# Loading bias, gate and expert weights at other places of a graph and expert network on one core

## What is computed

```python
# layer 3: graph attention, 4 heads of 64 channels
out = agg.reshape(n, H * C) + bias          # agg: weighted sum over each node's edges
x = x + elu(out)
# layer 4: 8 experts, the 2 with the best gate scores of each node
xn = layernorm(x)
gate_scores = xn @ Wg + bg
_, idx = top_k(gate_scores, 2)
h = gelu(xn @ W1[e] + b1[e]); y = h @ W2[e] + b2[e]     # for both experts, summed
x = x + y
```

## Time and profile before

| | |
|---|---|
| time, median of 3 runs | 6628.99 us (6628.88 to 6632.55) |
| span of the profiled execution, first to last instruction | 6628.2 us |
| busy: TensorE, VectorE, ScalarE, GpSimd | 71%, 60%, 30%, 64% |
| attention pass, its bulk | 3300 to 5400 us |
| routing pass | 5426.6 to 5756 us |
| expert pass | from 5784 us |

### The profile page before, as it was taken

The page is one execution under the profiler, slowest core; times in us unless marked ns, Lnnn a source line. Parts: engine busy times, 40 slices in busy tenths (PEclk is TensorE's granted clock), DMA queues, the critical chain, the costliest instruction groups (busy, mean ns, idle before and its releaser), DMA issues. The chain is left out here.

```text
span 6628.2 us, 114498 instructions
## 1 busy us (share of the span) xinstructions
PE 4704.7 (71%) x25073; PEld 4033.2 (61%) x25073; DVE 3983.4 (60%) x11854; ACT 1982.2 (30%) x4950; POOL 4262.0 (64%) x4656
## 2 busy tenths in 40 slices
PE   9965555555555558599276777776766767599997
PEld 4445555555555556599265656565655557599996
DVE  5565555555555559522577777777777768644442
ACT  3310000000000006133144444444444434366664
POOL 1257777777777767255677777777777738544443
PEclk9987777777777779699677777767777775599998
DMA  8843333333333339111444444444444435444445
GB/s 313 319 168 105 104 104 104 104 105 105 104 104 104 105 102 306 44 63 63 146 114 113 113 114 113 113 113 113 114 113 113 113 117 181 143 71 72 72 71 129
DMA packets 376353, 810.49 MB, mean 122 GB/s; under 512 B 88803, under 2 KB 234803, under 8 KB 362453
## 3 DMA queue, kind: packets, MB, share of 16 engines
q0 software_dynamic: 209712, 525.20, 30.1%
q1 hardware_dynamic: 138836, 160.68, 7.7%
q10 hardware_dynamic: 27568, 122.44, 5.0%
HBM read 578.58 MB, written 242.27 MB: 124 GB/s over the span
## 5 line engine op out<-in xcount | busy, mean ns | idle before, releaser
L1259 POOL DMA_INDIRECT s_rows<-xp_table,s_index x1664 | 1654.5, 994 | 507.1 <-issue 449.8
L347 POOL DMA_INDIRECT s_rows<-rel_table,s_staged x1664 | 1580.1, 950 | 520.0 <-issue 496.5
L373 PE MATMUL s_part<-s_pick,s_rows 128*128 128x128 f32 x6656 | 1198.0, 354 | 903.5 <-DMA s_rows<-rel_table,s_staged 704.3
L373 PEld LDWEIGHTS s_part<-s_pick,s_rows 128*128 128x128 f32 x6656 | 1109.8, 260 | 992.3 <-DVE s_pick L381 919.0
L1383 PE MATMUL s_part<-s_pick,s_scaled 128*128 128x128 f32 x6656 | 1422.3, 371 | 378.4 <-DVE s_scaled L1548 351.1
L1383 PEld LDWEIGHTS s_part<-s_pick,s_scaled 128*128 128x128 f32 x6656 | 1192.6, 263 | 575.0 <-issue 277.8
L394 DVE TENSOR_TENSOR sums<-sums,s_part 128x256 f32 x1666 | 702.0, 421 | 933.9 <-PE s_part L373 754.8
L1563 DVE SCALAR_TENSOR_TENSOR sums<-sums,s_old_share,s_part 128x256 f32 x1666 | 793.6, 476 | 418.7 <-PE s_part L1383 281.2
L1295 ACT ACTIVATE s_apart<-window,s_local 128x128 f32<-128x128 f32 x1664 | 531.6, 390 | 1148.9 <-PE s_part L1383 1087.9
L1548 DVE TENSOR_TENSOR s_scaled<-s_rows,s_share 128x256 f32<-128x256 f32 x1664 | 687.5, 413 | 74.6 <-issue 73.5
L2291 POOL DMA_INDIRECT sums_out<-s_y,s_ids x212 | 334.0, 1575 | 485.7 <-DVE s_ids L2400 470.7
(11 more groups left out here) (357 smaller groups left out, 5486.8 us busy)
## 6 DMA issues: line engine op xcount, KB each, us to landing
rel_table<-s_rows ACTq DMA_DIRECT2D x98, 1024.0 KB
s_rows<-exp_rows SPq DMA_DIRECT2D x212, 132.0 KB, 2.1
s_rows<-rel_table,s_staged POOLq DMA_INDIRECT x1664, 2.7
s_rows<-xp_table,s_index POOLq DMA_INDIRECT x1664
s_edges<-edge_rows SPq DMA_DIRECT2D x208, 80.0 KB
xp_table<-s_xp ACTq DMA_DIRECT2D x49, 264.0 KB, 3.9
s_x<-in_x SPq DMA_DIRECT2D x98, 128.0 KB, 4.2
s_x<-in_x SPq DMA_DIRECT2D x49, 256.0 KB
```

The lines of the kernel that those rows point to most:

```text
L347: pool.indirect_dma_start(out=rows[:, s, :], out_offset=None, in_=rel_table[:, :], in_offset=bass.IndirectOffsetOnAxis(ap=staged[:, 2 * s ...
L373: mm = pe.matmul(part[s % PARTS][:, k, :], rows[:, s, k * P:(k + 1) * P], pick[:, s % PICKS, :], start=True, stop=True)
L1259: pool.indirect_dma_start(out=rows[:, b * BATCH + s, :], out_offset=None, in_=xp_table[0:NP, :], in_offset=bass.IndirectOffsetOnAxis(ap=in ...
```

## The change

Three small tiles (gate weights, gate bias, attention bias: 26 floats in each partition) are allocated before the attention pass and kept, in place of tiles of the routing pass. SP loads them in the attention pass's block, after its last `follow`, with ten DMAs, and waits there for them; the waits of ScalarE, TensorE and VectorE in the routing pass are gone. The expert weights are no longer issued ahead of the pairs: in pairs 2, 6, ..., 30 SP issues the two loads of one expert, behind the load of x2 and ahead of the store of x3, and in pair 34 the load of `b2`. The expert pass waits for 17 loads instead of 3.

```diff
         sums = at(ctx, "sums8", [P, HALVES, NP + P])
+        wg = at(ctx, "gate_w", [P, HALVES, X])
+        bg = at(ctx, "gate_b", [P, X])
+        bias = at(ctx, "att_bias", [P, HALVES])
...
+                    def load_front():
+
+                        run = CH // HALVES
+                        for h in range(HEADS):
+                            for k in range(HALVES):
+                                sp.dma_start(bias[h * run:(h + 1) * run, k:k + 1],
+                                             a["att_bias"][0:1, h * CH + k * run:h * CH + (k + 1) * run].rearrange("o c -> c o")).then_inc(front_in, 16)
+                        sp.dma_start(wg[:, :, :], a["gate_w"]).then_inc(front_in, 16)
+                        sp.dma_start(bg[:, :], a["gate_b"].broadcast_to([P, X])).then_inc(front_in, 16)
...
                     with sp.Fori(0, BATCHES // 2 - 1) as i:
                         follow(i, 0)
                         follow(i, 1)
+                    load_front()
+                    sp.wait_ge(front_in, 16 * (HEADS * HALVES + 2))
...
-                    part = CH // HALVES
-                    for h in range(HEADS):
-                        for k in range(HALVES):
-                            sp.dma_start(bias[h * part:(h + 1) * part, k:k + 1],
-                                         a["att_bias"][0:1, h * CH + k * part:h * CH + (k + 1) * part].rearrange("o c -> c o")).then_inc(bias_in, 16)
+                    def load_expert(e):
+                        sp.dma_start(w1_b1[:, e, :], a["exp_w1_b1"][:, e, :]).then_inc(exp_in, 16)
+                        sp.dma_start(w2[:, e, :], a["exp_w2"][:, e, :]).then_inc(exp_in, 16)
+
                     load(0)
                     load(1)
-                    sp.dma_start(wg[:, :, :], a["gate_w"]).then_inc(w_in, 16)
-                    sp.dma_start(bg[:, :], a["gate_b"].broadcast_to([P, X])).then_inc(w_in, 16)
-
-                    sp.dma_start(w1_b1[:, :, :], a["exp_w1_b1"]).then_inc(exp_in, 16)
-                    sp.dma_start(w2[:, :, :], a["exp_w2"]).then_inc(exp_in, 16)
-                    sp.dma_start(b2[:, :, :].rearrange("p x d -> p (x d)"), a["exp_b2"].broadcast_to([P, X * D])).then_inc(exp_in, 16)
                     for q in range(PAIRS):
                         if q + 2 < PAIRS:
                             sp.wait_ge(part_done, q + 1)
                             load(q + 2)
+                        if q % 4 == 2 and q // 4 < X:
+                            load_expert(q // 4)
+                        if q == 4 * X + 2:
+                            sp.dma_start(b2[:, :, :].rearrange("p x d -> p (x d)"), a["exp_b2"].broadcast_to([P, X * D])).then_inc(exp_in, 16)
                         sp.wait_ge(x3_done, q + 1)
...
-                    act.wait_ge(bias_in, 16 * HEADS * HALVES)
...
-                    pe.wait_ge(w_in, 32)
...
-                    v.wait_ge(w_in, 32)
...
-                    act.wait_ge(exp_in, 48)
+                    act.wait_ge(exp_in, 16 * (2 * X + 1))
...
-                    v.wait_ge(exp_in, 48)
+                    v.wait_ge(exp_in, 16 * (2 * X + 1))
```

More of the change, by code:

```diff
@@ L1168, in gnn_kernel @@
             gathered = [sem(f"s8_gathered{b}") for b in range(2)]
-            cleared = sem("s8_cleared")
+            cleared, front_in = sem("s8_cleared"), sem("s8_front_in")
             rows_scaled, apart_done, picked, product, added = (sem(f"s8_{n}") for n in ("rows_scaled", "apart_done", "picked", "product", "added"))
@@ L1761, in gnn_kernel @@
         with ExitStack() as st:
-            wg = at(st, "s9_wg", [P, HALVES, X])
-            bg = at(st, "s9_bg", [P, X])
-            bias = at(st, "s9_bias", [P, HALVES])
             x2 = at(st, "s9_x2", [P, 2, 2, D])
@@ L1794, in gnn_kernel @@
             psR = [bank(st, f"s9_psR{b}", 2, X) for b in range(2)]
-            w_in, bias_in = sem("s9_w_in"), sem("s9_bias_in")
             x_in, x3_out = [sem(f"s9_x_in{b}") for b in range(2)], [sem(f"s9_x3_out{b}") for b in range(3)]
```

## The result

The changed kernel takes 6606.82 us (median of six runs, 6603.35 to 6608.56); the kernel before takes 6629.86 us in the same measurement (six runs, 6624.70 to 6633.03). The ratio is 0.9965, 95% interval 0.9954 to 0.9977: faster by 0.35%, 23.0 us. Forecast were 22.3 us, and 6606.7 us as the time.

What follows compares the result with a forecast made beforehand. GpSimd was taken to bound the routing pass from its first scatter, so only that scatter's start counts: 5.1 (opening) + 17.2 (stall) + 0 (weights) = 22.3 us, 6629.0 - 22.3 = 6606.7 us; range 6602 to 6613.

Steps and rivals of the forecast that it cites:

- GpSimd as the bound, 5.8 us a pair: Routing pass from its first scatter on: GpSimd has no holes and sets the pace, 5.8 us a pair.
- Opening, 5.1 us: Start of the routing pass: no wait for bias and gate loads, VectorE's first add 5.1 us earlier (4.2 to 5.4).
- The second condition: VectorE's first add also needs x2 of pair 0, issued 4.24 us earlier and landing at 5428.7 to 5430.3.
- Stall, 17.2 us: Add of pair 2: the 18.13 us wait for x2 behind the expert weights goes, ScalarE is late next, gain 17.2 us.
- Weights beside the pairs, 0: Routing pass: expert loads among the pairs cost 0; one expert takes 5.9 us beside the steady traffic.
- lead: Loads of x2 in the routing pass: an expert can take about 13.3 us before VectorE waits.
- The other bound, 26 us of stretched issues: GpSimd's scatters: one issue in each of nine loads stretched by 2.9 us, 26 us in all; held unlikely.
- Small loads in the attention pass, 0: End of the attention pass: ten more issues, 5.3 us of an SP that then idles over 100 us, cost 0.
- Cut up: Rival, routing pass: each ninth of the weights delays its pair, only the opening's gain remains, 6623.9 us; chance 0.07.
- the opening gains nothing: Rival, start of the routing pass: ScalarE or x2 is late for another reason, 6611.8 us; chance 0.05.
- exposed in full: Rival, routing pass: pairs stand still for the small expert loads, 52 us, time 6659 us; chance 0.02.
- gathers by their address: Rival, attention pass: tile addresses move by about 100 bytes and stretch gathers, up to 78 us; chance 0.03 for well slower.

Runs made afterwards that it cites:

- kernel 8: Changed kernel with each inverse root computed a second time on GpSimd into an unread tile; 7924.1 us, ratio to the kernel before 0.9998.
- kernel 4: Changed kernel with all expert weights issued in pair 2 as seventeen loads; 8085.6 us, ratio to the kernel before 0.9983.
- kernel 10: Changed kernel with expert weights put back as three whole loads ahead of the pairs, run again on chip C; 8095.2 us, one run.
- kernel 12: The kernel before the change, unaltered, run again on chip C for a trace; 8095.8 us, one run.
- kernel 2: Kernel before with only the expert weights moved beside the pairs, bias and gate loads as before; 8081.8 us, ratio to the kernel before 0.9980.
- kernel 1: Changed kernel with expert weights put back as three whole loads ahead of the pairs, on chip A; 8088.5 us, ratio to the kernel before 0.9989.
- kernel 3: Changed kernel with all expert weights issued in pair 2 as three whole loads; 8082.6 us, ratio to the kernel before 0.9980.
- kernel 6: The changed kernel, unaltered, run again on chip B; 7898.6 us, ratio to the kernel before 0.9962.
- kernel 11: Changed kernel with the inverse root moved from GpSimd to ScalarE as exp of a logarithm; 8103.7 us, ratio to the kernel before 1.0014.

## Why the prediction was right, point by point

- **GpSimd as the bound, 5.8 us a pair: right.** Stretch 281.8 us after; kernel 8 lengthens it by 0.7 of the added work, with hardly any idle time filled.
- **Opening, 5.1 us: right in size, and the reason for the choice too.** The first add moved from 8.24 to 2.97 us after the first issue, 5.3 us. The second condition that the prediction named, x2 of pair 0, is now what it waits for (1.67 us), landing inside the forecast window of 5428.7 to 5430.3 counted from the old start. The page after now has a landing for these loads, 2.8 us at the median, between the two rows of 2.1 and 3.7 us that the forecast went by.
- **Stall, 17.2 us: right.** F - S fell by 22.5 us; less the opening's 5.3 this leaves 17.2. The add of pair 2 waits 0.88 us for ScalarE, 18.13 - 0.88 = 17.25. It is the stall minus what was late next that counts.
- **Weights beside the pairs, 0: right, though the lead was put too long.** 286.7 against 287.2 us on one chip, and 283.4 against 281.8 on the first. The DMA share is 0.70 in a window with weights, as forecast. There is a lead, and it has the order forecast: with 1.05 MB a burst no pair waits, with 4.2 MB one waits 3.6 us, with 9.45 MB 16.4. At pair 2 it is 10.0 us by the forecast's own reckoning and not 13.3, and a burst drains more slowly than at 424 GB/s. A burst of one expert is too short for either to matter. The other bound, 26 us of stretched issues, did not occur: the 196 scatters take 195.2 us in all, and took 196.8.
- **Small loads in the attention pass, 0: right.** SP issues them in 4.6 us, 109 us before the pass ends.
- **Rivals.** "Cut up" falls with the stretch; "the opening gains nothing" with the first add; "exposed in full" with the missing waits and with kernel 4, where seventeen loads cost 0.6 us of wait; "gathers by their address" with 993 for 994 ns. The block does start 0.5 us earlier than at 5426.6, which the prediction called a sign of the gathers; it is too little to bear on the verdict.
- **How near the number came is in part luck.** The 22.5 us of the first scatter fit the 22.3 of the sum. The 0.5, 1.6 and -1.1 us beside them were not forecast and mostly cancel, and the interval of the ratio allows 15 to 30 us.
- **What the prediction did not say:** that the two parts aren't independent. It adds 5.1 and 17.2 as though each stood alone. The sum is right for both together. For one alone the split is about 3 and 19: 3.0 us for the front (kernels 10 and 12, one run of a trace each) and 43.8 - 24.8 = 19.0 for the weights, of which the second number crosses chips.

Open: kernel 2's stretch is 298.2 us where kernel 1 on the same chip has 293.6. Its scatters aren't slower (199.9 us in all for 200.6); GpSimd is idle ahead of scatters and powers for 66.7 us instead of 61.6, 4.5 of these 5.1 us in waits for VectorE, and VectorE itself sits longer ahead of `s_counts` (32.9 us for 21.2). Chip C has such waits in the kernel before too (24.7 us), with no weights beside the pairs, and chip B shows no cost of the weights (286.7 to 287.2). One trace of each doesn't tell chance from a few us of contention on the slower chips. Also open is why the DMA engines ran at 369 GB/s in kernel 10 and at 384 in kernel 12.

## What to carry to other kernels

A small load that stands in a queue behind megabytes waits for all of them, whoever needs them. Compare a burst with the lead of the loads behind it (here 10 to 13 us, two pairs), count the traffic that goes beside it, and cut until it fits. Cutting finer cost little here: seventeen loads for three, 0.6 us of wait. When a stall goes, subtract what is late next. And when two edits sit on one chain, ask what each is worth alone: ahead of a wait for a transfer, work that is done earlier gains only what the end of the transfer gains.

## What the runs showed of the hardware

- **SP can be held in issuing.** Behind the expert weights one store took 7.8 us to issue (kernel 12), 9.8 (kernel 10) and 13.4 (kernel 3), where the same instruction takes 0.36 us in the steady pass. In these kernels no load of x2 was due behind it. In kernel 4 one was: VectorE was through with pair 3 at 6892.86, and the load of x2 for pair 5 went out at 6903.18, behind the seventeen issues of weights and a store. What makes an issue long is not shown beyond that all long ones stand behind megabytes.

```profile
6897.79 13.37 SPq L1831 DMA_DIRECT2D sums_out<-s_x  x1
```

```profile
6903.18 2.34 SPq L1818 DMA_DIRECT2D s_x<-x_rows  x1
```

- **Many loads in a queue cost about as much as few.** 9.45 MB took 30.1 us in three loads and 30.7 us in seventeen, up to the landing of what stood behind them.
- **The issue of an indirect DMA on GpSimd is no constant.** Its median is 0.96 to 0.98 us everywhere, but its mean goes from 984 ns (kernel 8) to 1020 (kernel 6) on one chip and to 1056 (kernel 11) on another, with single ones of over 1.4 us. The length of a pair doesn't explain it: pairs are longer than kernel 6's in both kernel 8 and kernel 11. What stretches them was not shown.
- **Ln and Exp in turn reload their tables each time,** 1.28 us a load in kernel 11; Relu, Exp and Copy in turn do so nowhere in its routing pass.
- **Chips differ** by 20% on this kernel (6.6 to 8.1 ms) through the gather passes, and the routing pass by up to 4% (283 to 295 us for the scatters of the kernel before). Differences inside a stage carried over; the kernel's total time didn't.
